# Tap logits with swapped roles: four column strips of TensorE, a copy by ScalarE and two transposes

## The reference, cut to what matters

```python
a = jax.nn.relu(_bn(jnp.einsum('oi,bic->boc', se_att_w1, kq), se_att_bn))    # 81 rows
a = jnp.einsum('oi,bic->boc', se_att_w2, a) + se_att_b2[None, :, None]       # 9 logits
a = jax.nn.softmax(a, axis=1)
out1 = jnp.einsum('bcdhw,bdc->bchw', v_win, a) + k1
...
a2 = jax.nn.softmax(a2.reshape(bs, SPA_HEAD, hw), axis=-1)                   # spatial branch
```

## Time and profile before

| what | us |
|---|---|
| three runs, median (lowest to highest) | 1727.88 (1720.87 to 1733.21) |
| the profiled execution | 1718.95 |
| its span, first to last instruction | 1717.2 |
| the mixer's stretch | about 380 to 820 |
| PE busy over the span | 1312.7 |
| DVE busy over the span | 1151.7 |
| ACT busy over the span | 803.2 |

### The profile page before, as it was taken

One profiled execution on the slowest core, in us unless ns is written; L12 is line 12 of the kernel. 1 busy time (PEld: TensorE's weight loads), 2 busy tenths in 40 slices (PEclk: granted clock), 3 DMA queues, 4 the chain that ended last, 5 costly groups with the idle time before them and its releaser, 6 DMA issues.

```text
span 1717.2 us, 38603 instructions
## 1 busy us (share of the span) xinstructions
PE 1312.7 (76%) x9764; PEld 1104.1 (64%) x9765; DVE 1151.7 (67%) x3074; ACT 803.2 (47%) x1779; POOL 653.3 (38%) x561
## 2 busy tenths in 40 slices
PE   0297898979999999997555553799999999999200
PEld 0286888865666666666555553688888888888200
DVE  7795333327886877866588888466666666666493
ACT  0293444435444544543799995333333333333350
POOL 0162111113433434332266766254554544544200
PEclk9997887879998989986555555899999999999655
DMA  8535544569889789892233335232332232322575
GB/s 311 133 90 194 193 161 164 192 185 211 189 169 214 170 177 201 181 183 54 95 123 126 123 123 167 80 89 89 89 92 89 84 93 87 94 89 72 209 294 248
DMA packets 265629, 254.48 MB, mean 148 GB/s; under 512 B 152608, under 2 KB 240804, under 8 KB 261562
## 3 DMA queue, kind: packets, MB, share of 16 engines
q1 hardware_dynamic: 245285, 200.93, 43.2%
q0 software_dynamic: 20320, 53.28, 9.6%
HBM read 156.03 MB, written 105.57 MB: 152 GB/s over the span
## 4 chain that ended last, share of the span: by engine, by line
PE 57%; DVE 19%; ACT 7%; DMA 6%; issue 5%; SPq 3%; DVEq 1%; ACTq 0%; POOLq 0%; POOL 0%
PE ps L700 14%; PE ps L685 13%; PE ps L503 5%; PE ps L469 4%; DMA u_d<-in_zstrings 2%; ACT pool_ L1265 2%; PE ps L669 2%; DVE big L1221 2%; PE ps L550 2%; PE ps L533 2%; DVE pool_ L1213 2%; SPq L280 2%; PE ps L485 2%; PE ps L535 2%; ACT big L1347 1%
## 5 line engine op out<-in xcount | busy, mean ns | idle before, releaser
L1492 POOL DMA_INDIRECT y_d<-pool_,to_s x176 | 254.9, 1449 | 283.0 <-DVE pool_ L1181 247.3
L700 PE MATMUL ps<-pool_,aux 128*128 x2112 | 248.3, 274 | 5.6 <-DVE aux L1173 3.2
L685 PE MATMUL ps<-aux,pool_ 128*128 128x256 f16 x2112 | 246.0, 273 | 0.8 <-ACT aux L1393 0.6
L700 PEld LDWEIGHTS ps<-pool_,aux 128*128 128x128 f16 x2112 | 198.3, 98 | 50.1 <-issue 24.8
L685 PEld LDWEIGHTS ps<-aux,pool_ 128*128 x2112 | 205.9, 98 | 25.5 <-issue 1.6
L1393 ACT ACTIVATE aux<-ps,b_s 128x256 f32<-128x256 f32 x352 | 138.4, 475 | 162.0 <-DVE aux L1173 160.1
L1472 POOL DMA_INDIRECT rows_d<-aux,idx_s x162 | 160.3, 990 | 105.4 <-DVE idx_s L1084 56.1
L1181 DVE SCALAR_TENSOR_TENSOR pool_<-ps,pool_ 128x512 f32<-128x512 f32 x88 | 60.9, 692 | 140.1 <-PE ps L700 140.1
L1464 POOL DMA_DIRECT2D pool_<-v_d x64 | 50.1, 783 | 234.0 <-PE ps L581 232.6
L1385 ACT ACTIVATE aux<-ps 128x512 f16<-128x512 f32 x88 | 52.5, 597 | 172.9 <-PE ps L669 172.8
L1173 DVE TENSOR_TENSOR aux<-aux 128x1024 f16<-128x1024 f32 x88 | 107.9, 1226 | 3.1
(11 more groups left out here) (204 smaller groups left out, 3168.3 us busy)
## 6 DMA issues: line engine op xcount, KB each, us to landing
pool_<-rows_d SPq DMA_DIRECT2D x88, 258.0 KB
pool_<-y_d SPq DMA_DIRECT2D x18, 1152.0 KB, 8.7
big<-in_x SPq DMA_DIRECT2D x2, 5184.0 KB, 20.9
xn_d<-big SPq DMA_DIRECT2D x16, 648.0 KB, 3.0
v_d<-aux SPq DMA_DIRECT2D x64, 162.0 KB, 2.0
ks_d<-aux SPq DMA_DIRECT2D x64, 162.0 KB, 1.9
pool_<-ks_d SPq DMA_DIRECT2D x64, 162.0 KB, 3.3
pool_<-xn_d SPq DMA_DIRECT2D x64, 162.0 KB, 4.1
```

The costliest lines, as they stand in the source:

```text
L685: last = nc.tensor.matmul(o, w_s[:, a, bass.ds(e * (4 * PIECE) + (k * HID + j * 128), 128)], xh_s[:, par, b, k * SLOTS:(k + 1) * SLOTS], s ...
L700: last = nc.tensor.matmul(ps[:, 6 + par, s * C:(s + 1) * C], hh_s[:, par, a, j, s * 128:(s + 1) * 128], w_s[:, b, bass.ds(e * (4 * PIECE) ...
L1492: nc.gpsimd.indirect_dma_start(out=y_d[:, :], out_offset=bass.IndirectOffsetOnAxis(ap=to_s[:, par, k:k + 1], axis=0), in_=yo_s[:, par, k, ...
```

## The change

The operands of `tap_logits` change roles. The nine tap columns, padded to 32, become the stationary operand and the hidden map (256 channels) streams past: one matmul per image instead of two. The four images' results go to four strips of 32 output partitions in bank 0, so that the four matmuls use four strips of 32 columns of the array. The result has taps on partitions and channels along the free axis. ACT copies it to SBUF as one 128 by 256 tile, and after `spatial_2` PE transposes its two halves back to channels on partitions (`turn_logits`, banks 2 and 3). `pixel_maximum` on DVE now waits for both `spatial_2` matmuls and for the transposes before its first maximum, and its copy reads two banks. `keys` waits in addition for ACT's copy of the group before, since both use bank 0.

```diff
-        se_w2_s = sb("se_w2_s", [HW + 1, D])
+        se_w2_s = sb("se_w2_s", [HW + 1, 32])
...
+        tl_s = take(128, 2, C)
...
                     pe.wait_ge(S["a_c"], 2 * g)
+                    pe.wait_ge(S["tl_c"], g)
...
                 pe.wait_ge(S["a_c"], 2 * g + 2)
                 pe.wait_ge(S["a2_c"], 2 * g + 1)
-                for j in range(G * 2):
-                    last = nc.tensor.matmul(ps[:, 2, TOK + j * D:TOK + (j + 1) * D],
-                                            a_s[:, par, j // 2, (j % 2) * 128:(j % 2 + 1) * 128],
-                                            se_w2_s[:, :], start=True, stop=True)
+                for b in range(G):
+                    last = nc.tensor.matmul(ps[32 * b:32 * b + 32, 0, 0:C], se_w2_s[:, :], a_s[:, par, b, :],
+                                            start=True, stop=True)
+                last.then_inc(S["tl_p"], 1)
+
+            def turn_logits(g, par):
+
+                pe.wait_ge(S["tl_c"], g + 1)
+                for h in range(HALVES):
+                    last = nc.tensor.transpose(ps[:, 2 + h, TOK:TOK + 128], tl_s[:, par, h * 128:(h + 1) * 128],
+                                               ident_s[:, :])
                 last.then_inc(S["lg_p"], 1)
...
                     spatial_2(2 * i)
+                    turn_logits(2 * i, 0)
...
                     spatial_2(2 * i + 1)
+                    turn_logits(2 * i + 1, 1)
...
             def pixel_maximum(g, par):
 
+                dve.wait_ge(S["l2_p"], g * 2 + 2)
+                dve.wait_ge(S["lg_p"], g + 1 + CREDIT)
                 for h in range(HALVES):
-                    dve.wait_ge(S["l2_p"], g * 2 + h + 1)
                     ins = nc.vector.reduce_max(sm_s[:, par, 0, h * G:(h + 1) * G],
                                                ps[:, 2 + h, 0:TOK].rearrange("p (b n) -> p b n", b=G), axis=AX.X)
 
-                dve.wait_ge(S["lg_p"], g + 1 + CREDIT)
-                ins = nc.vector.tensor_copy(lg_s[:, par * G * 2:(par + 1) * G * 2, :],
-                                            ps[:, 2, TOK:TOK + G * 2 * D].rearrange("p (j d) -> p j d", d=D))
+                ins = nc.vector.tensor_copy(
+                    lg_s[:, par * G * 2:(par + 1) * G * 2, :].rearrange("p (b h) d -> p h b d", h=HALVES),
+                    ps[:, 2:4, TOK:TOK + 128].rearrange("p h (b d) -> p h b d", d=32)[:, :, :, 0:D])
...
                         act.wait_ge(S["sa1_p"], g * 2 + h + 1)
                         nc.scalar.activation(a2_s[:, h, :], ps[:, 2 + h, 0:TOK], ACT.Relu, bias=sa_ab[:, h, 1:2],
                                              scale=sa_ab[:, h, 0:1]).then_inc(S["a2_c"], 1)
+                    act.wait_ge(S["tl_p"], g + 1)
+                    nc.scalar.activation(tl_s[:, par, :], ps[:, 0, 0:C], ACT.Copy).then_inc(S["tl_c"], 1)
                     if par == 0 and not first:
                         residues(i - 1)
```

More of the change, by code:

```diff
@@ L244, in metaformer_kernel @@
                    rk_in1 mb_p mb_e0 mb_e1 tq_p pt_c cv_p v_c ks_c r1_c st_v0 st_v1 st_v2 st_v3 ch_d ch_g kq_in0
-                   kq_in1 c_in0 c_in1 v_in0 v_in1 t_c se1_p a_c lg_p lgs_c ex_c ar_c arx_c raw_p msk_c sa1_p a2_c
+                   kq_in1 c_in0 c_in1 v_in0 v_in1 t_c se1_p a_c tl_p tl_c lg_p lgs_c ex_c ar_c arx_c raw_p msk_c sa1_p a2_c
                    l2_p l2m_c e_c band_p x1_c phase_a wst_in0 wst_in1 wst_in2 whi_c wlo_c b2_in rm_p rw_c xs_c
@@ L1565, in halves @@
         return np.ascontiguousarray(a.reshape(HALVES, 128, -1).transpose(1, 0, 2))
-    se_w2 = np.concatenate([i["conv_se_att_w2"].T, i["conv_se_att_b2"][None]], 0)
+    se_w2 = np.zeros((HW + 1, 32), f)
+    se_w2[:, 0:D] = np.concatenate([i["conv_se_att_w2"].T, i["conv_se_att_b2"][None]], 0)
     wx, wk = i["conv_se_att_w1"].T.reshape(2, HW, HW)
```

## The result

The changed kernel takes 1744.50 us (median of seven, 1742.46 to 1750.50), the kernel before 1729.55 (seven, 1715.17 to 1733.95): recorded ratio 1.0105, 95% interval 1.0069 to 1.0142.

The account below looks back on a forecast made before the run. The prediction took a chain alternating between DVE's leg and PE's odd half as the bound, not PE alone. Fifteen turns by 0.37 (5.5 us) plus 4 from the clock, say 10, off 1728 gave 1718; range 1697 to 1742.

Parts of the forecast that it names:

- The strips: Tap logits in the odd half: four column strips run side by side, 0.43 us in all, upper end 1.72.
- rival 1: Strips overlap by one only, each second pass beside the next one's first: 1.08 us instead of 0.43, 1720 total; chance 0.20.
- rival 2: Strips run in a row, 1.72 us or more, so the kernel is slower: 1742, or 1768 with whole latencies; chance 0.18.
- The odd half's sum: From the old tap logits' place to DVE's copy L875: 3.12 us against 3.49, 0.37 saved per turn.
- the entry of 0.10: PE going into the mode of small tiles before the tap logits: 0.10 us, an estimate, ends 0 and 0.19.
- The exit: PE leaving the mode of small tiles after the tap logits: 0.19 us, from 0.15 + 0.10 less 0.07.
- The even half: PE waits 1.1 us ahead of L562 for residues; later work comes 0.4 later, absorbed by slack ahead of L573.
- DVE's leg, taken as unchanged: Odd L871 to the next even one, DVE's own work: 14.57 us, with no change counted in the sum.
- Rival 4: Little change: L871 starts earlier, but DVE's leg stretches by meeting GpSimd's work and the clock stays: 1728; chance 0.12.
- The clock, 4 us won: Denser streaming in L550's place shortens slow-clock stretches in the mixer: 4 us saved, an estimate between 0 and 24.
- the prediction's own sign of being wrong: Strips of over 0.8 us, or a mean clock in the mixer off 0.92 by more than 0.02 either way.
- Rival 3: PE's two waits bring a clock fall into every turn: ten more turns add 24, less 5.5: 1747; chance 0.08.

## Why the prediction was wrong

Forecast: 1718, faster by 10; measured: slower by 15. Step by step:

- **The strips** (0.43, all four at once): right: 0.57 to the next matmul, exit included. The rule weighed against them, from the Trainium skill, "TensorE: Matmul & The Clock Gate", section "Part 3: Packing small matmuls", that weight loads pass a running matmul only where the row groups differ, does not hold in this trace as far as the recorded starts go: four first passes start together in strips that share all their rows, and the second passes after them. The same section gives three column tiles a speed-up of 2.38, which the prediction left out and which points the way this trace went. Whatever the starts, 0.57 is less than the 1.08 of rival 1 and the 1.72 of rival 2; both fall with it.
- **The odd half's sum** (3.12 from the strips' place to the copy): 564.17 - 561.17 = 3.00 from the first strip, and spatial_1 to the first strip grew by the entry of 0.10 (2.38 for 2.28): 3.10. Right. (The exit, put at 0.19, adds up to 0.18 from its own terms, which changes nothing.) Its worth, 0.37 per turn, is 0.30 with GpSimd's operations out of the way (23.15 against 23.45): right in kind, 0.07 too large. The even half takes some back: there the band now starts 3.10 after the maxima, before 3.00.
- **The even half** (L562, now L571, 0.4 later and PE waiting 1.1, absorbed): about right, PE waits 0.87. The slack named for it was 0.9 to 2.3, where 2.3 is a wait of weight loads; PE's own longest was 1.89.
- **DVE's leg, taken as unchanged**: wrong. The 14.57 of the earlier trace rows mixes two views; by the timeline that leg is 616.90 - 602.41 = 14.49, which is also the median. It became 15.00, 8.4 us in all, because the same GpSimd operations now meet L914 and L917. Rival 4 names this cause, but prices it at the gain only. The term needed a bound: the longest form of these steps.
- **The clock, 4 us won**: wrong in sign; this is the main step that failed, DVE's leg the second. I counted what denser work in L550's place would give a stretch that is already slow (that it shortens such a stretch, no run shows), and took the number of falls as given. The falls rose from 7 to 12 of 14 turns, 16 us, since PE's wait ahead of the band grew from 1.89 to 2.66 and now comes in all 14 turns instead of 10. The mean clock of 0.88 is the prediction's own sign of being wrong (off 0.92 by more than 0.02). Rival 3, with a chance of 0.08, gave 1747 by this mechanism; that it comes so near is in part luck, since it has ten more falls, not five, and no loss in DVE's leg. The wait ahead of the band is the one that counts: lengthened in the kernel before, where PE waits ahead of its transposes only once, it brought a fall into every turn, and the one ahead of L571 remained in the run with the filler and brought none.

What the 0.65 per turn more from GpSimd comes from is read from the ends of the rows above: DVE's steps meet the same two operations earlier in their course. What stays open is why a wait brings a fall in one turn and not in the next: before, 3 of the 10 waits of 1.89 brought none, and in the changed kernel 2 of 14.

## What to carry to other kernels

In this kernel an engine made faster off the end of the chain turned its time into waiting, and where that engine is TensorE the wait had a price: the granted clock of what comes after. Before counting a gain on PE, write down how long it will then stand and where, and if the chain's other leg belongs to DVE, look there first; a filler of matmuls in the wait is a cheap test (here the ratio to the kernel before went from 1.0105 to 0.9907). Steps of DVE in SBUF that show two durations for one shape (0.83 and 2.07) point to GpSimd beside them, and moving one of its operations to ACT and holding the other back by a wait of a few us was worth more (2.8% in the kernel before) than the change studied.

## What was not expected of the hardware

- Waits of PE of 1.9 to 2.9 us were enough for the clock to fall to its lower level: in 7 of 14 turns before (after 7 of the 10 waits of 1.89), 12 in the changed kernel (2.66), 14 with the lengthened leg (2.85 in most), none with 0.82. The length alone doesn't decide: two waits of 2.66 brought no fall.
- A fall costs more than the wait that brings it: in the changed kernel legs from even to odd 3.2 to 4.8 us longer after waits of 2.2 to 2.7.
- Column strips that share all their rows run side by side in float32: eight passes of 256 columns in 0.57 us, where one pass alone streams for 0.215, an estimate from 324 columns, and eight in a row would be 1.72.
- Two DVE maxima that read PSUM were not slowed by GpSimd's addition in SBUF (0.89 with it and without), a DVE sum of 128 by 648 in SBUF was (2.07 for 0.83).
- A stretched DVE step ends at a fixed distance from the end of the GpSimd operation that it met: 0.42 before the scaling's end (14 steps in each of the two kernels), 0.69 after the addition's (10 before, 14 changed).
